# Attention and eight experts in one program: last entries on VectorE, first weights and gather inside attention, alternating score banks, last norm in the experts' block

## The reference

```python
q, k, v = (proj(w) for w in (w_q, w_k, w_v))            # 16 heads of 16
probs = softmax(einsum('bhqd,bhkd->bhqk', q, k) / 4)
x = layernorm(x + einsum('bsd,ed->bse', attn(probs, v), w_o))
gates = softmax(x_flat @ gating_w)                      # 4096 rows, 8 experts
topk_w, topk_idx = top_k(gates, 2)                      # weights over their sum
position = cumsum(onehot(flat_e))[item] - 1             # capacity 1280 per expert
h = relu(einsum('ecd,edh->ech', buf, w1) + b1)          # hidden 1024
out_e = einsum('ech,ehd->ecd', h, w2) + b2
x = layernorm(x + scatter_add(flat_t, out_e[...] * w_eff))
```

## Time and profile before

| what | value |
|---|---|
| median of 3 runs | 980.37 us (977.14 to 990.34) |
| profiled execution | 981.65 us, its span 979.8 us |
| TensorE busy | 846.6 us (86%) |
| VectorE, ScalarE, GpSimd busy | 561.8, 461.4, 431.8 us |
| attention | 0 to about 450 us |
| experts | about 453 to 950 us |
| last norm | from 952.76 us |

### The profile page before, as it was taken

One profiled execution on the slowest core, in us unless ns is written; L12 is line 12 of the kernel. 1 busy time (PEld: TensorE's weight loads), 2 busy tenths in 40 slices (PEclk: granted clock), 3 DMA queues, 4 the chain that ended last, 5 costly groups with the idle time before them and its releaser, 6 DMA issues. The chain is left out here.

```text
span 979.8 us, 19547 instructions
## 1 busy us (share of the span) xinstructions
PE 846.6 (86%) x7441; PEld 753.7 (77%) x7441; DVE 561.8 (57%) x1151; ACT 461.4 (47%) x851; POOL 431.8 (44%) x636
## 2 busy tenths in 40 slices
PE   5579889999999997840999999999999999999940
PEld 4466667677777765540999999999999999999940
DVE  3356647777777786241455666565555545666415
ACT  3036646666666665311344444444444444444316
POOL 2000215555656555474144545444444444545225
PEclk8579989999999999665899999999999999999985
DMA  5755967676775551014123444343442524322229
GB/s 127 101 80 79 246 126 117 106 119 115 116 113 97 90 108 28 23 44 152 34 45 87 88 91 87 48 95 84 93 87 43 130 45 86 87 44 46 26 35 334
DMA packets 74807, 90.75 MB, mean 93 GB/s; under 512 B 10428, under 2 KB 61788, under 8 KB 74588
## 3 DMA queue, kind: packets, MB, share of 16 engines
q1 hardware_dynamic: 57308, 68.47, 33.2%
q0 software_dynamic: 17408, 21.05, 13.2%
HBM read 37.87 MB, written 25.84 MB: 65 GB/s over the span
## 5 line engine op out<-in xcount | busy, mean ns | idle before, releaser
L1014 POOL DMA_INDIRECT acc_rows<-o_w,lists x80 | 136.5, 1706 | 242.0 <-ACT o_w L1065 229.8
L672 DVE TENSOR_REDUCE negm<-wide 128x4 f32<-128x1024 f32 x128 | 156.2, 1220 | 65.5 <-PE wide L787 65.3
L1143 PE MATMUL wide<-g_hi,w_hi 128*128 128x256 f32 x640 | 184.3, 288 | 0.0
L1145 PE MATMUL wide<-g_hi,w_lo 128*128 128x256 f32 x640 | 181.0, 283 | 0.0
L1144 PE MATMUL wide<-g_lo,w_hi 128*128 128x256 f32 x640 | 180.8, 282 | 0.0
L1162 PE MATMUL bank<-w_lo,h_hi 128*128 128x256 f32 x640 | 180.1, 281 | 0.0
L1161 PE MATMUL bank<-w_hi,h_hi 128*128 128x256 f32 x640 | 180.1, 281 | 0.0
L1163 PE MATMUL bank<-w_hi,h_lo 128*128 128x256 f32 x640 | 179.8, 281 | 0.0
L1055 ACT ACTIVATE h<-wide,b1T 128x256 f32<-128x256 f32 x320 | 132.9, 470 | 71.3 <-DVE h_hi L1098 53.2
L488 ACT ACTIVATE probs<-wide 128x1024 f32<-128x1024 f32 x128 | 131.0, 1024 | 74.0 <-PE wide L802 70.8
L1065 ACT ACTIVATE o_w<-o_b,lists 128x256 f32<-128x256 f32 x80 | 36.3, 502 | 193.6 <-DVE o_b L1111 193.6
(11 more groups left out here) (162 smaller groups left out, 1510.4 us busy)
## 6 DMA issues: line engine op xcount, KB each, us to landing
stack<-qk SPq DMA_DIRECT2D x96, 256.0 KB, 8.1
w_raw<-in_L_ffn_w SPq DMA_DIRECT2D x16, 1024.0 KB, 5.9
x_sb<-in_L_attn_x SPq DMA_DIRECT2D x16, 256.0 KB, 8.6
x_rows<-x SPq DMA_DIRECT2D x16, 256.0 KB, 4.1
acc_rows<-x SPq DMA_DIRECT2D x16, 256.0 KB, 4.4
acc_sb<-acc_rows SPq DMA_DIRECT2D x8, 512.0 KB, 7.5
out<-out_sb SPq DMA_DIRECT2D x8, 512.0 KB, 3.7
x_rows<-zrow SPq DMA_DIRECT2D x1, 1280.0 KB, 11.8
```

The source lines that it names most:

```text
L672: nc.vector.tensor_reduce(negm[n % 2][:, :, :, u].rearrange("p c x -> p x c"), SQ[:, :, :].rearrange("p x (c t) -> p x c t", c=QC), X, ALU ...
L1014: nc.gpsimd.indirect_dma_start(out=acc_d, out_offset=bass.IndirectOffsetOnAxis(ap=lists[:, e, QC * c + r, 0:1], axis=0), in_=o_w[c][:, r, ...
L1143: nc.tensor.matmul(out, w1_hi[:, k, f], G_hi[:, k, :], start=(k == 0), stop=False)
L1145: ins = nc.tensor.matmul(out, w1_lo[:, k, f], G_hi[:, k, :], start=False, stop=(k == DK - 1))
```

## The change

Six things are changed.
1. Score blocks 0 to 10, which run before any shifted score, use the two bank pairs in turn and wait only for the maximum before the last one; shifted scores of blocks 118 to 127, which run after the last plain score, do the same with the exponentials.
2. The entries of sequences 12 to 15 (was: 14 and 15) are made on VectorE; `dest` and `item` have four buffers instead of two. The offsets CH, POS and LIST are 52, 54 and 58 (were 54, 55 and 59), ScalarE's step of CH comes a turn later, and VectorE does the split of the maxima ahead of `chosen`.
3. Zero fills and first weights are issued in turn 142 instead of 40, weights first.
4. The buffers of the first weights' parts, of the gathered rows and of the lists lie in the space of `stack`. ScalarE and VectorE split expert 0's weights at the end of the attention block. SP loads the list of expert 0 and then the others there, and GpSimd gathers block 0 of expert 0 there.
5. In the experts' block b2 and later weights are loaded a little later (they wait for transposes); layer 1 of the first block runs before the transposes of the second. The last block is done in two halves of 128 rows, in two banks: bias, weighing and add-back of the first half wait only for it; all add-backs wait row group by row group.
6. The last norm is part of the experts' block, works in place, and takes four adjacent rows per partition (4 KB) instead of rows 128 apart.

The diff, cut to its core:

```diff
+        stack = [sb(f"stack{i}", [P, H // 2, 2, S], F32R) for i in range(3)]
+        space = [t[:, :, :, :].rearrange("p u w t -> p (u w t)") for t in stack]
+        w1_hi, w1_lo = (space[1][:, i * DK * FF:(i + 1) * DK * FF].rearrange("p (k f) -> p k f", k=DK) for i in range(2))
+        w2_hi, w2_lo = (space[2][:, i * FT * D:(i + 1) * FT * D].rearrange("p (f d) -> p f d", f=FT) for i in range(2))
+        rows = [space[0][:, c * QC * D:(c + 1) * QC * D].bitcast(F32).rearrange("p (r d) -> p r d", r=QC) for c in range(NC)]
+        lists = space[0][:, NC * QC * D:NC * QC * D + NE * BLK * 2].bitcast(I32).rearrange("p (e j w) -> p e j w", e=NE, w=2)
...
-        dest = [sb(f"dest{i}", [P, QC, TOPK], I32) for i in range(2)]
-        item = [sb(f"item{i}", [P, QC, TOPK, 2], I32) for i in range(2)]
+        dest = [sb(f"dest{i}", [P, QC, TOPK], I32) for i in range(4)]
+        item = [sb(f"item{i}", [P, QC, TOPK, 2], I32) for i in range(4)]
...
-        UT, AT, O, LN, X1, X1T, LG, CH, POS, LIST = 35, 37, 38, 41, 45, 46, 49, 54, 55, 59
+        UT, AT, O, LN, X1, X1T, LG, CH, POS, LIST = 35, 37, 38, 41, 45, 46, 49, 52, 54, 58
         LAST = 8 * (NB - 1) + LIST + 2
-        TAIL = NB - 2
+        TAIL, LTAIL = NB - 2, NB - 4
+        ALONE, LEFT = ST0 - S0, PAIRS * (NB - 1) + S0 - ST0 + PAIRS + 1
...
+        def score_banks(i):
+
+            return SD if i < ALONE and i % 2 else SQ
+
+        def shifted_banks(i):
+
+            return SQ if i >= LEFT and i % 2 else SD
...
+                if turn == 8 * (NB - 1) + MT + 2:
+                    sp.dma_start(g["w1_raw"][:, :, :], g["w1_d"][0].rearrange("(c p) f -> p c f", p=P)).then_inc(g["w1_loaded"], 16)
+                    sp.dma_start(g["w2_raw"][:, :, :], g["w2_d"][0].rearrange("(f p) d -> p f d", p=P)).then_inc(g["w2_loaded"], 16)
                     zeros = zrow[:, :].unsqueeze(1).to_broadcast([P, BLK, D])
                     sp.dma_start(x1_d[T:T + TRASH, :].rearrange("(j p) d -> p j d", p=P), zeros).then_inc(filled, 16)
                     sp.dma_start(acc_d[T:T + TRASH, :].rearrange("(j p) d -> p j d", p=P), zeros).then_inc(filled, 16)
-                    sp.dma_start(g["w1_raw"][:, :, :], g["w1_d"][0].rearrange("(c p) f -> p c f", p=P)).then_inc(g["w1_loaded"], 16)
-                    sp.dma_start(g["w2_raw"][:, :, :], g["w2_d"][0].rearrange("(f p) d -> p f d", p=P)).then_inc(g["w2_loaded"], 16)
...
             for i in range(2):
                 sp.wait_ge(x1_stored[i], 32 * (NB // 2))
-                sp.wait_ge(listed[i], 16 * QC * TOPK * (NB // 2))
+            for i in range(4):
+                sp.wait_ge(listed[i], 16 * QC * TOPK * (NB // 4))
             sp.wait_ge(filled, 48)
+            sp.dma_start(lists[:, 0].rearrange("p j w -> p (j w)"), list_v[:, 0]).then_inc(g["list0_loaded"], 16)
+            sp.dma_start(lists[:, 1:].rearrange("p e j w -> p e (j w)"), list_v[:, 1:]).then_inc(g["lists_loaded"], 16)
 
...
-                m = due(turn, LIST, TAIL)
+                m = due(turn, LIST, LTAIL)
...
+            pool.wait_ge(g["list0_loaded"], 16)
+            for r in range(QC):
+                nc.gpsimd.indirect_dma_start(
+                    out=g["rows"][0][:, r, :], out_offset=None, in_=x1_d,
+                    in_offset=bass.IndirectOffsetOnAxis(ap=lists[:, 0, r, 0:1], axis=0)).then_inc(g["gathered"][0], 16)
...
-                    nc.scalar.activation(probs[:, i % 4].rearrange("p x c t -> p x (c t)"), SD[:, :, :], ACT.Exp,
+                    nc.scalar.activation(probs[:, i % 4].rearrange("p x c t -> p x (c t)"), shifted_banks(i)[:, :, :], ACT.Exp,
                                          scale=SCALE).then_inc(exp_done, 1)
-                m = due(turn, CH, NB)
+                m = due(turn, CH + 1, NB)
                 if m is not None:
...
+            act.wait_ge(st_ready, PAIRS * NB)
+            act.wait_ge(g["w1_loaded"], 16)
+            for i in range(PARTS):
+                f = slice(i * (FF // PARTS), (i + 1) * (FF // PARTS))
+                nc.scalar.activation(g["w1_hi"][:, :, f], g["w1_raw"][:, :, f], ACT.Copy).then_inc(g["w1_hi_done"], 1)
+            act.wait_ge(g["w2_loaded"], 16)
+            for i in range(PARTS):
+                f = slice(i * (FT // PARTS), (i + 1) * (FT // PARTS))
+                nc.scalar.activation(g["w2_hi"][:, f, :], g["w2_raw"][:, f, :], ACT.Copy).then_inc(g["w2_hi_done"], 1)
...
-                if m is not None and m >= TAIL:
+                if m is not None and m >= LTAIL:
...
+                n = due(turn, MT, NB)
+                if n is not None:
+                    dve.wait_ge(mT_hi_done, n + 1)
+                    nc.vector.tensor_tensor(mT_lo[:, :], banks[BB][0:H, 0:S], mT_hi[:, :].bitcast(F32),
+                                            ALU.subtract).then_inc(mT_lo_done, 1)
...
-                pe.wait_ge(max_done, i)
+                if i == 1:
+                    pe.wait_ge(wT_lo_done, 4)
+                pe.wait_ge(max_done, max(i - 1, 0) if i < ALONE else i)
+                out = score_banks(i)
                 for c in range(QC):
                     for x in range(2):
                         k = slice(HALF * x, HALF * x + KEYS)
-                        ins = nc.tensor.matmul(SQ[:, x, c * S:c * S + S], st[k, u, 0, c * P:c * P + P], st[k, u, 1, :],
...
-                pe.wait_ge(exp_done, i)
+                pe.wait_ge(exp_done, i - 1 if i > LEFT else i)
+                out = shifted_banks(i)
+                if out is SQ:
...
-            sp.dma_start(lists[:, :, :, :].rearrange("p e j w -> p e (j w)"), list_v).then_inc(lists_loaded, 16)
+            sp.wait_ge(gT_ready, 1)
             sp.dma_start(b2_all[:, :, :].rearrange("p e d -> p (e d)"), b2_d.rearrange("e d -> (e d)").partition_broadcast(P)).then_inc(b2_loaded, 16)
             for e in range(1, NE):
+                sp.wait_ge(gT_ready, NC * (e - 1) + 3)
...
+            for i in range(NG):
+                sp.dma_start(a[:, i], acc_v[i]).then_inc(acc_loaded[i], 16)
+            for i in range(NG):
+                sp.wait_ge(out_done, GROUP * (i + 1))
+                sp.dma_start(out_v[i], a[:, i]).then_inc(stored, 16)
...
-                pool.wait_ge(ow_done, QC * (NC * e + c + 1))
                 if c == 0 and e > 0:
                     for i in range(NC):
                         pool.wait_ge(added[i], 16 * QC * e)
                 for r in range(QC):
...
+                if n == LASTN:
+                    dve.wait_ge(half_ready, 1)
+                    nc.vector.tensor_tensor(o_b[c % 2][:, 0, :], bank(BO[c % 2], a=QC)[:, 0, :], b2_all[:, e, :], ALU.add).then_inc(half_biased, 1)
+                    dve.wait_ge(eo_ready, n + 1)
+                    nc.vector.tensor_tensor(o_b[c % 2][:, 1, :], bank(BO[1 - c % 2], a=QC)[:, 1, :], b2_all[:, e, :], ALU.add).then_inc(ob_done, 1)
+                    return
...
+                    last = n == LASTN and r == 1
+                    if last:
+                        pe.wait_ge(ob_done, n)
+                    out = bank(BO[1 - c % 2 if last else c % 2], a=QC)[:, r, :]
                     for f in range(FT):
...
-    split(split_w1, 0)
-    split(split_w2, 0)
     take_in(0, 0)
+    layer1(0, 0)
     take_in(0, 1)
-    layer1(0, 0)
     for e in range(NE):
...
-    acc_v = acc_d[0:T, :].rearrange("(g t p) d -> g p t d", p=P, t=GROUP)
...
+    acc_v = acc_d[0:T, :].rearrange("(g p t) d -> g p t d", p=P, t=GROUP)
```

202 lines of the change are left out of this document (97 added, 105 removed).

## The result

The changed kernel took **966.16 us** (median of 9 runs, 959.52 to 974.67) against 976.83 us for the kernel before (9 runs): ratio 0.990, 95% interval 0.985 to 0.995. The ratio leaves out the slow executions, over 1.5% above the fastest of their kernel: two of the changed kernel, the profiled one among them, and one of the kernel before. Two later groups of runs on other chips gave 0.986 [0.982, 0.989] and 0.985 [0.982, 0.988]. So the gain is 11 to 16 us, where 24.8 us were forecast. 956 us was nearly met (959.1 and 957.4 us in the later groups), but that is luck: the kernel before is also faster than the 980.4 us that the forecast stood on, 972.8 to 976.8 us on these chips.

The account below looks back on a forecast made before the run. TensorE was taken as busy without a gap in the experts, so only places around its dense stretches could gain. Terms -1.7 - 8.2 + 0 - 2 - 3.5 - 3.6 - 5.8 = -24.8 us gave 956 us; range 948 to 968.

Parts of the forecast that it names:

- The step that failed: TensorE's dense stretches in attention and the experts (474.1 us) keep all their matmuls, so gains lie only around them.
- its sign of being wrong: The forecast is wrong if the places around the dense stretches gain and the stretch of the experts grows.
- Start, -1.7: Start of attention: alternating bank pairs remove waits for row maxima; -1.7 us, between 0 and -4.
- Transfers, -8.2: Hole near 120 us: moving zero fills and first weights from turn 40 to 142 gives -8.2 us, range -4 to -8.5.
- Rival C: The turn-40 hole comes back or the transfers disturb later rows: 4 to 5 of the 8.2 us lost, 961 us; chance 0.10.
- Loop order, 0: Attention loop: choosing experts two turns earlier nets 0 us, from -2 to +4.
- rival B: The loop's new order costs 14 us, 970 us; sign: mean transpose distance above 22.3 us, sequences 5 to 12; chance 0.10.
- End of attention, -2: End of attention: alternating banks remove ScalarE waits of shifted scores and exponentials; -2 us, from 0 to -6.
- entries, -3.5: Last sequences' entries: relieving GpSimd and the wait at dest ends the last scatter earlier; -3.5 us, from -5.5 to -1.
- rival A: VectorE's weight splits hold up GpSimd's last scatters, which end 4.8 us later: 961 us; chance 0.06.
- Passage, -6.1 and +2.5: Passage to the experts: transposes 6.1 us sooner after the last scatter, +2.5 us for block 1's late g_lo; net -3.6 us.
- The end, -5.8: After the last block: split block, no change of block, and 4 KB rows give -5.8 us, from -4 to -7.5.

Follow-up runs that it names:

- e2: The changed kernel with 640 unused bytes per partition ahead of the experts' own tiles; 956.31 us, ratio 0.982 to the kernel before.
- e8: The kernel before with its lists allocated behind the experts' other tiles; ratio 1.005 to the kernel before.
- e16: e10 with 32 unused bytes in place of 640 ahead of the experts' tiles and 32 more ahead of h_hi; 944.62 us, ratio 0.970.
- e14: The kernel before with the shift rows sent as two transfers of two rows; 969.85 us, ratio 0.997.
- e1: The changed kernel as it is, run again on another chip; 959.11 us, ratio 0.986 to the kernel before.
- e15: The changed kernel as it is, run again beside e13 and e14; 957.37 us, ratio 0.985 to the kernel before.
- e5: e2 without the alternation of score bank pairs at both ends of attention; 957.04 us, ratio 0.981 to the kernel before.
- e3: The kernel before with only the zero fills and first weights moved from turn 40 to turn 142; 963.45 us, ratio 0.992.
- e9: e2 with the attention loop's old order (choice of experts, position matmuls and lists at turns 54, 55, 59); ratio 0.983 to the kernel before.
- e6: e2 with the transposes of the experts' block 1 between two halves of layer 1 of block 0; 950.13 us, ratio 0.975.
- e13: The changed kernel with the shift rows sent as two transfers of two rows; 954.75 us, ratio 0.981 to the kernel before.
- e10: e6 with the shift rows as two transfers of two rows instead of four of one row; 946.16 us, ratio 0.966 to the kernel before.

## Why the prediction was wrong

**The step that failed** is the first: "Nothing in the change takes matmuls out of either stretch", so the experts' 474 us got no term. The number of matmuls did stay, but not what one takes. The change puts the first weights' parts, rows and lists where attention's stacks were; the 640 bytes of lists no longer lie between the weights and g and h, and each matmul starts 119.9 ns after the last instead of 118.6. 96 matmuls a block x 1.3 ns = 0.125 us; the rows have 0.13, and 38 blocks make 4.9 of the 5.05 us. Shown: e2 takes it away with one unused tile, e8 brings it into the kernel before with one moved line, e16 goes 0.13 us per block beyond. The prediction had named this as its sign of being wrong: the places gain and the stretch of the experts grows.

Taking before and e14 against after, e1 and e15, where nothing else is said, the other steps:
- **Start, -1.7.** 53.1 against 50.9 us: 2.2 earlier. Over all profiles it is 1.3 (see e5), so the size is right within their spread, and it is not shown to last beyond sequence 0.
- **Transfers, -8.2.** Right: 8.1 us in e3, and the distance 29.91 to 21.38. Rival C, which leaves 3 to 4 us, lies below e3's interval.
- **Loop order, 0.** Right in the sum in e1 and e15. It gives 0.2 us in each undisturbed sequence; the mean distance from sequence 5 to 12 is 22.1 us in e1 and e15. In the first profile of the changed kernel it is (316.85 - 153.55) / 7 = 23.3, past the sign that I had set for rival B, but the two sequences with drops of the clock hold 10.6 of the 12.9 us above 21.48, and e9 has such drops with the old order.
- **End of attention, -2, and entries, -3.5.** In the profile before the granted clock was low from 388 to 411 us (0.50); in e8 and e14 it falls only after 402 us. They took 120.1 and 119.9 us for the whole stretch, e1 and e15 117.1 and 118.1: about -2.5. Both terms were too large. From the transposes of sequence 12 to y of 15, a row that all kernels have, it is 96.3 to 97.0 us in e3, e8 and e14 and 95.5 and 96.6 in e1 and e15. From there to the last scatter's end it is 23.97 us before (447.66 - 423.69), 23.2 to 23.8 in e3, e8 and e14, and 21.4 to 21.7 in all kernels with the change: -2.1 where -3.5 were forecast. The forecast end, 443.7 to 444.1, lies 20.0 to 20.4 us behind y. The weights of 15 came as forecast (14.5 us behind y, forecast 14.8), but the last twelve scatters took 16.4 to 16.6 us, where it was 15.16. Two of the scatters of 15 took 1.19 and 1.97 us beside VectorE's splits, 1.2 us more than the others, in every kernel with the change and in none without. That is a quarter of rival A, whose chance the prediction put at 0.06; the strict reading of the Trainium skill (SBUF — State Buffer, Who interferes with whom) would have given 4.8 us.
- **Passage, -6.1 and +2.5.** List and gather were quicker: 2.10 us from the list's issue to the first gather, where I used 2.8 (the Trainium skill, DMA: Bandwidth & Descriptors, Anatomy of one DMA, gives 2.0 us, a fit for transfers that GpSimd issues; SyncE issues this one, and the row agrees all the same). The change of block was slower, 5.71 us after the last gather's end, like the 5.55 us behind the last scatter before (453.21 - 447.66); I had let landing and change overlap, and no such gain shows. Net -5.5 (20.54 to 15.07). The order of the first steps costs 2.3 to 4.8 us where 2.5 were forecast: the wait of 1.95 us was near, the block's transposes on the path and a clock of 0.72 from 467 to 472 us came on top. e6 wins back 3.9.
- **The end, -5.8.** Right in each part: 3.81 to 1.48, 6.75 to 3.82, load to statistics 4.05 to 3.50, in all -5.9 to -6.2.
- **The base.** The terms were differences to one profile of 981.65 us that spent some 8 us more in the end of attention than e8 and e14. Part of what the changed kernel "gains" there is this one execution.

Of the shortfall of some 10 us (24.8 against ratios of 0.985 and 0.986), 5.0 are placement, about 3 the end of attention with the entries, 0.6 the passage and 1.3 the order of steps; the last three are differences of few profiles. Late shift rows are 0 to 1.5 us of it by the times of e13 to e15. The first nine executions fell short by 4 us more; their mean clock was 0.928, against 0.935 in e1 and 0.934 in e15, and no run shows why. Open stays why the shift rows are late in sequences 5 and 10 above all, and why the transposes of 12 to 15 take 60 us in some profiles and 64 to 67 in others; no run was made for either.

## What to carry to other kernels

When a change moves tiles, ask what the new addresses do to matmuls in stages that it doesn't touch, and compare the distance of two repeating rows, which reads to 0.1%, before comparing medians. Where terms of one stage are checked, measure from a row that both kernels have: absolute times carry along what earlier stages won or lost. And take the base for a forecast from several runs, and ask of a low clock in a profile whether it belongs to the kernel or to that execution.

## What was not expected of the hardware

- The distance between matmul starts depends on where the tiles of g and h lie (to the weights or by themselves, no run tells): 119.9 ns where their offset to the weights is a multiple of 256 bytes, 118.6 at 128 bytes, 116.7 at 32 bytes in layer 1. Weight loads read 192 ns in the change and in e8, 188 ns before. The transposes of the gathered rows kept 272 ns in both.
- Waits of 0.6 to 1.8 us of TensorE in the middle of dense work were in many cases followed by a granted clock of 0.5 (1.2 GHz) for 2 to 10 us: 6.2 us lost in the sequence of 162.78 (27.64 against 21.48 us between transposes), 2.5 us in e1 after 0.6 us, nothing after 1.16 us at 203.05. In the first nine runs the spans went from 957.8 to 972.9 us, span times mean clock only from 893.6 to 897.9: the spread of the times is the clock's.
- A transfer of two shift rows is issued in 0.55 to 0.57 us (e10), one of one row in 0.62 to 0.75: half as many more than halve the queue's time.
